# One expert tile is formed in the last batch, and its gate and up products stand between the products of the last routing chain

## The reference

```python
x = norm(x + attention(x, wq, wk, wv, wo, rel_pos))          # 32 heads of 8, a bias by distance
x = norm(x + mamba(ctx_1024, z=x))                           # 16 states, a scan over 256 steps, gated by silu(x)
x = norm(x + ffn(x))

# the third part, for 1024 tokens and 4 experts
probs = softmax(x @ Wr + br); top_w, top_idx = top_k(probs, 1)
h = silu(x @ Wg[e]) * (x @ Wu[e])      # 256 -> 1024, for the token's own expert e
out = (h @ Wd[e]) * top_w              # 1024 -> 256
```

## Time and profile before

| | |
|---|---|
| median of 3 runs | 472.5 us (472.37 to 473.3) |
| the profiled execution, its own time | 473.93 us |
| its span | 472.2 us |
| PE busy | 420.8 us (89%) |
| DVE busy | 312.3 us (66%) |
| POOL busy | 221.1 us (47%) |
| ACT busy | 211.2 us (45%) |
| chain that ended last: PE, DVE, POOL, issue | 66%, 17%, 6%, 5% of the span |

### The profile page before, as it was taken

The page is one execution under the profiler, slowest core; times in us unless marked ns, Lnnn a source line. Parts: engine busy times, 40 slices in busy tenths (PEclk is TensorE's granted clock), DMA queues, the critical chain, the costliest instruction groups (busy, mean ns, idle before and its releaser), DMA issues.

```text
span 472.2 us, 7846 instructions
## 1 busy us (share of the span) xinstructions
PE 420.8 (89%) x2560; PEld 212.2 (45%) x2561; DVE 312.3 (66%) x626; ACT 211.2 (45%) x412; POOL 221.1 (47%) x246
## 2 busy tenths in 40 slices
PE   4989588878998998989989899986999999999993
PEld 3444222333443443444434444354556666666652
DVE  3497778999987878878888786588214333334344
ACT  2456717564664557745577457612121111112220
POOL 2000615877986679967799578600551111111001
PEclk9998765798999999999999999999999999999997
DMA  9689940937365182756324430079120000000000
GB/s 237 91 279 108 301 144 12 146 119 115 89 138 110 68 134 70 134 180 199 137 78 169 159 112 0 1 287 361 55 55 11 12 4 9 11 11 11 11 1 9
DMA packets 39366, 49.36 MB, mean 105 GB/s; under 512 B 4664, under 2 KB 32673, under 8 KB 39334
## 3 DMA queue, kind: packets, MB, share of 16 engines
q1 hardware_dynamic: 36322, 46.65, 39.0%
q0 software_dynamic: 1056, 2.10, 1.5%
q10 hardware_dynamic: 1956, 0.21, 0.4%
HBM read 40.72 MB, written 8.91 MB: 105 GB/s over the span
## 4 chain that ended last, share of the span: by engine, by line
PE 66%; DVE 17%; POOL 6%; issue 5%; DMA 3%; ACT 2%; POOLq 0%; SPq 0%; DVEq 0%; ACTq 0%
PE ps L1181 16%; PE ps L1197 8%; PE ps L883 8%; PE ps L910 6%; PE ps L914 5%; PE ps L956 4%; PE ps L783 4%; DVE arena L1572 3%; DVE arena L1523 3%; DVE arena L1505 3%; PE ps L943 3%; PE ps L1189 2%; DMA arena<-arena 2%; POOL arena L655 2%; POOL arena L661 2%
## 5 line engine op out<-in xcount | busy, mean ns | idle before, releaser
L1372 ACT ACTIVATE arena<-ps 128x512 f32<-128x512 f32 x128 | 76.1, 595 | 84.9 <-PE ps L943 84.7
L1523 DVE TENSOR_REDUCE arena<-ps 128x2 f32<-128x512 f32 x128 | 86.6, 681 | 26.8 <-PE ps L914 22.7
L661 POOL TENSOR_TENSOR arena<-arena 128x512 f32<-128x512 f32 x60 | 76.8, 1279 | 36.2 <-DVE arena L1572 36.2
L655 POOL TENSOR_TENSOR arena<-arena 128x512 f32<-128x512 f32 x64 | 84.4, 1321 | 9.0 <-issue 8.8
L1181 PE MATMUL ps<-arena 128*128 x176 | 77.5, 593 | 0.7 <-ACT arena L1413 0.7
L1572 DVE TENSOR_TENSOR_SCAN arena<-ps,arena 128x512 f32<-128x512 f32 x60 | 72.8, 1214 | 0.5 <-DVE mv L1617 0.2
L883 PE MATMUL ps<-arena,identf 128*128 128x512 f32 x128 | 68.9, 625 | 0.0
L910 PE MATMUL ps<-arena 48*128 48x256 bf16 x256 | 52.7, 288 | 13.4 <-DVE arena L1523 10.0
L1331 ACT ACTIVATE ps<-arena 128x255 f32<-128x255 f32 x128 | 60.4, 473 | 1.9 <-DVEq L1726 1.9
L1839 DVE TENSOR_TENSOR arena<-arena,ps 128x1024 f32<-128x1024 f32 x11 | 13.4, 1222 | 59.9 <-ACT arena L1417 59.9
L731 POOL DMA_INDIRECT out<-rows_s,arena x11 | 10.8, 984 | 88.7 <-DVE rows_s L1868 80.5
(11 more groups left out here) (231 smaller groups left out, 524.7 us busy)
## 6 DMA issues: line engine op xcount, KB each, us to landing
arena<-bc_d SPq DMA_DIRECT2D x32, 512.0 KB, 4.4
arena<-in_L_ffn_Wg SPq DMA_DIRECT2D x8, 512.0 KB, 6.1
arena<-in_L_ffn_Wu SPq DMA_DIRECT2D x8, 512.0 KB, 5.9
arena<-in_L_ffn_Wd SPq DMA_DIRECT2D x4, 1024.0 KB, 11.7
arena<-kp_d SPq DMA_DIRECT2D x8, 384.0 KB, 7.9
arena<-qp_d SPq DMA_DIRECT2D x8, 384.0 KB, 10.8
qp_d<-arena SPq DMA_DIRECT2D x4, 384.0 KB, 8.5
kp_d<-arena SPq DMA_DIRECT2D x4, 384.0 KB, 8.4
```

The lines of the kernel that those rows point to most:

```text
L655: g.tensor_tensor(dBu[m % 3], dtu[:, :, b * SEQ:(b + 1) * SEQ], over_k(bcr[c % BC_RING][:, m % 2, 0, :]), ALU.mult).then_inc(dbu_ready, 1)
L661: g.tensor_tensor(h, h, over_k(bcr[m // 2 % BC_RING][:, m % 2, 1, :]), ALU.mult).then_inc(hc_ready, 1)
L1372: A(prob[2 * (slot % 2) + kt][:, pr * HALF:(pr + 1) * HALF], ps[:, 2 + n % 2, :], ACT.Exp).then_inc(p_ready, 1)
L1523: v.tensor_reduce(negm[b % 2][:, qt, 2 * pair:2 * pair + 2], ps[:, bank, :].rearrange("p (h k) -> p h k", h=2), axis=AX.X, op=ALU.max).the ...
```

## The change

The first two batches hold 4 token tiles, 512 tokens. With 4 experts at least one has 128 or more of them. The change picks the first such expert (`estar`) in the last batch, gives its first 128 tokens slot 0, and routes all other tokens to the slots from 1 on. Slot 0's rows are picked before the end of the routing, and its gate and up are cut into four halves of 4 records each, which stand between the products of the last chain. The number of slots stays 11.

```diff
@@ POOL: the constants stand 7 scans earlier, with 4 memsets more
-                if m == 3 * STATES + 8:
+                if m == 3 * STATES + 1:
                     routing_constants()
-            for s in (1, 0, 2):
+            for s in (2, 0, 1):
                 gather(s)
-            hand_row(1)
+            hand_row(2)
@@ PE
+                        if b == BATCH - 1 and (qd, i) == (3, 0):
+                            count_early()
...
+            pe.wait_ge(y_out, BATCH)
+            pick_rows(EARLY, early_rows, early_ready)
             pe.wait_ge(x2_ready, 2 * (BATCH - 1))
             turn_late(BATCH - 2)
...
-            keep_warm(2, 5)
+            pe.wait_ge(wgu_in, 16 * 16)
+            pe.wait_ge(xcur_ready, 2)
+            first_expert = pe.value_load(estar_int[0:1, 0:1], min_val=0, max_val=EXPERTS - 1)
+            gate_up_half(0, first_expert)
             route_late(BATCH - 1)
-            keep_warm(10, 7)
+            for half in (1, 2):
+                gate_up_half(half, first_expert)
...
             mm(ps[:, 6, 0:EXPERTS * TT], ones_b, oh_cols, start=True, stop=True).then_inc(count_pe, 1)
-            keep_warm(14, 4)
+            gate_up_half(3, first_expert).then_inc(gu_done, 1)
+            keep_warm(4, 4)
...
-            pe.wait_ge(wgu_in, 16 * 16)
-            gate_up(0, first_expert)
-            turn_x(1)
-            keep_warm(8, 6)
             turn_h(0)
@@ ACT
+            take_x(0)
             put_late(0)
@@ DVE, in the last batch
+                        if b == BATCH - 1 and (qd, i) == (2, 1):
+                            dve.wait_ge(taken, turns.count)
+                            early_experts()
+                        if b == BATCH - 1 and (qd, i) == (3, 0):
+                            early_counts()
+                        if b == BATCH - 1 and (qd, i) == (4, 0):
+                            early_choice()
+                        if b == BATCH - 1 and (qd, i) == (5, 0):
+                            early_ranks()
+                        if b == BATCH - 1 and (qd, i) == (6, 0):
+                            early_marks()
@@ DVE, after the loop
+            link(v.tensor_tensor(e_of[:, 0:1], e_of[:, 0:1], estar, ALU.add))
```

More of the change, by code:

```diff
@@ L50 @@
 SLOTS = TT + EXPERTS - 1
+EARLY = TT // 2
 EPS = 1e-5
@@ L1027, in route, with count_early @@
                 last.then_inc(turned, 1)
+            def count_early():
+                pe.wait_ge(early_oh, 1)
+                pe.wait_ge(consts, 4)
+                bank = turn()
+                n = EXPERTS * EARLY
+                mm(ps[:, bank, 0:n].rearrange("p (e t) -> p e t", e=EXPERTS), ltri, ohb[:, :, 0:EARLY], start=True, stop=True)
+                mm(ps[:, bank, n:2 * n].rearrange("p (e t) -> p e t", e=EXPERTS), ones_b, ohb[:, :, 0:EARLY], start=True,
+                   stop=True).then_inc(turned, 1)
             pe.wait_ge(consts, 3)
@@ L1096, in expert_of, with gate_up_half, pick_rows @@
                 return pe.value_load(e_int[0:1, bass.ds(s, 1)], min_val=0, max_val=EXPERTS - 1)
+            def gate_up_half(half, e):
+                w, fh = (wg_s, wu_s)[half // 2], half % 2
+                for k in range(KT):
+                    last = mm(ps[:, half, :], xcur[:, k, :], w[:, bass.ds((e * KT + k) * DFF + fh * HALF, HALF)],
+                              start=(k == 0), stop=(k == KT - 1))
+                return last
+            def pick_rows(tiles, marks, ready):
+                for t in range(tiles):
+                    pe.wait_ge(ready, t + 1)
+                    for k in range(KT):
+                        last = mm(ps[:, 7, k * P:(k + 1) * P], xres[:, t, k * P:(k + 1) * P], marks[t],
+                                  start=(t == 0 and k == 0), stop=(t == tiles - 1), skip_group_check=True)
+                last.then_inc(xt_pe, 1)
             def turn_late(b):
@@ L1147, in _ @@
             mm(ps[:, 6, 0:EXPERTS * TT], ones_b, oh_cols, start=True, stop=True).then_inc(count_pe, 1)
-            keep_warm(14, 4)
+            gate_up_half(3, first_expert).then_inc(gu_done, 1)
+            keep_warm(4, 4)
             pe.wait_ge(x2_ready, TT)
[L1151 to L1156, removed]
+            pick_rows(TT, first_rows, first_ready)
             pe.wait_ge(expert_ready, 1)
-            first_expert = expert_of(0)
             for t in range(TT):
@@ L1177, in gate_up @@
                 pe.wait_ge(xcur_ready, s + 2)
[L1178 to L1183, removed]
+                for half in range(4):
+                    last = gate_up_half(half, e)
                 last.then_inc(gu_done, 1)
@@ L1711, in _ @@
+            def early_marks():
+                for t in range(EARLY):
+                    v.tensor_scalar(early_rows[t], lanes, float(P + 1), lane1[:, t:t + 1], ALU.add,
+                                    ALU.is_equal).then_inc(early_ready, 1)
             dve.wait_ge(ld_route, 32)
```

95 lines of the change are left out of this document (74 added, 21 removed).

## The result

The changed kernel takes 481.27 us (median of 4 runs, 479.62 to 483.43) against 472.75 us (4 runs of the kernel before beside it): a ratio of 1.0182, with an interval of 1.0139 to 1.0226. The forecast was 474.7 us, with a range up to 477.5. The direction was right, the size was not: 8.5 us in place of 2.2.

A forecast was written before the change was run, and what follows sets the result against it. The prediction took the chain to run through PE, and through small DVE operations before 334 us. Batch cost 9.25 less end gain 7.0 made it 2.25 us longer: span 476.2, median 474.7 us, range 467.8 to 477.5.

The forecast's parts named there:

- The gain of the end, 7.0 us: From the routing chain to slot 1: gate and up start at about 338.0, not 345.07; gain between 6.6 and 8.0.
- The conflict: Last batch: small DVE operations wait for POOL's 1.27 us products, so the batch takes 9.25 us, not 3.4; chance 0.45.
- My rule, two inputs in SBUF: Last batch: an inserted DVE operation with both inputs in SBUF lasts until the running POOL product of 1.27 us ends.
- The stalls: Last batch, PE late at inserted DVE work: 2.75 us in quad 2, 1.4 in quad 3, 3.1 in quad 4.
- quads 5 and 6: Last batch: seven operations and four marks take 4.7 us against 2.70 idle on DVE, so 2.0 us late.
- PE is 2.75 us late: Quad 2 of the last batch: the copy ends at 271.2, making PE 2.75 us late in place of 1.0.
- 3.1 us late: Quad 4 of the last batch: the copy ends at 284.6, making PE 3.1 us late in place of 1.0.
- The load of the expert's number takes the place of two fillers and I give it nothing: Routing chain on PE, before the first half's products: the load was priced at zero.
- The signs: Expected in the profile: index to slot 1 2.8 us, counts scan 1.2 us later, PE standing 1.1 us in quad 3.
- 1.2 us of cover: Ahead of the router's products: last Wu lands by 319.1, at most 7.9 us after issue, 1.2 us before PE comes.
- rivals: Small operations free, 468.9, chance 0.27; each mark waits, 476.4, 0.13; all hidden, 465.5, 0.08; others, including late weights, 0.07.
- Each mark waits: Quad 6 of the last batch: each mark waits for its own POOL product, 3.7 us late, 476.4 us; chance 0.13.

The follow-up runs named there:

- 5: Kernel of 2 with a separate semaphore for Wg's loads, so the first half of gate and up waits for Wg alone: 473.10 us, ratio 1.0003.
- 8: Kernel of 7 plus the separate semaphore for Wg's loads and 8 PE fillers ahead of the turn of slot 0: 467.62 us, ratio 0.9889.
- 9: Kernel of 8 with PE's load of the expert's number moved ahead of the 12 fillers: 467.14 us, ratio 0.9864.
- Experiment 3: Changed kernel without four of POOL's products beside the inserted operations of quads 2 and 4: 474.01 us, ratio 1.0039.
- experiment 1: Changed kernel with unused PE filler products ahead of two last-batch waits, 11 in quad 2, 16 in quad 4: 475.46 us, ratio 1.0066.
- 2: Kernel of experiment 1 with 8 more PE fillers ahead of the turn of slot 0: 475.00 us, ratio 1.0046.
- 7: Changed kernel with three groups of its DVE operations moved to places where DVE was idle, constants at m = 52: 470.89 us, ratio 0.9961.
- 6: Changed kernel without its part in the last batch, constants back at m = 56, expert 0 and zero rows for slot 0: 470.76 us, ratio 0.9948.
- experiment 4: Kernel before with only the early routing in the last batch, results unused, old end kept: 485.49 us, ratio 1.0293.

## Why the prediction was wrong

- **The gain of the end, 7.0 us: right as a path, paid late.** With its waits away it is 6.9 (5, 8). In the changed kernel it was 5.9 to the start of slot 1 and 3.9 with the slower products of slot 1. With the load out of the way as well it is 7.9 (9), near the upper bound of 8.0.
- **The conflict: right.** The second inserted operation of quad 2 was to last about 1 us and took 0.74, the third, a copy, 1.19. In quad 4 I named the second and fourth; it was the second and the third, a scalar operation. Experiment 3 shows POOL's products as the cause. My rule, two inputs in SBUF, was too narrow, since the copy and the scalar operation have one. The Trainium skill ("SBUF — State Buffer", section "Who interferes with whom") lists copies and `tensor_scalar` as operations that can enter a two-port mode and contend then; the trace agrees, with 1.19 against 0.17 us.
- **The stalls: right.** Quad 2: the scores start 3.94 us behind the turned maxima in place of 1.30, 2.6 late (forecast 2.75). Quad 3: 0.94 (1.4). Quad 4: 3.54 in place of 0.61, 2.9 late (3.1). That makes 6.5; by experiment 1 it is 7.0 up to the turned maxima of quad 4, where I had 7.25, and 0.3 for all that is behind them, where I had 2.0 for quads 5 and 6. The ranks met no product at all, and DVE's slack hid the marks even at 3.73 us. (In quad 2 the prediction says that six operations remain behind the two that wait; there are seven, and its 270.8 counts seven.)
- **The step that failed: in the terms "PE is 2.75 us late" and "3.1 us late" a stall was priced at its own length.** In the kernel before no stall from the turned maxima of quad 2 to the end of the loop is longer than 0.92 us and its clock is 1.00 there, so I took the products behind a stall at their old duration, and had no rival in which they are slower. Behind 2.58, 3.54 and 1.93 us they ran at the lower clock, and in the batch that was 6.6 us, about as much as the stalls themselves (1). Behind the turn it was 0.9 for the turn and 2.0 for slot 1. The whole difference, for the span: the forecast's chain grew by 2.25 us, the measured one by 9.5. Of these 7.3 us (7.25 before rounding), 6.6 are the clock in the batch, 2.0 the slower slot 1 and 1.1 the end (0.9 of it the slower turn); against them stand 0.2 from the stalls, 1.7 from quads 5 and 6, and the 0.4 us of lead. The Trainium skill ("TensorE: Matmul & The Clock Gate", section "HAM oscillation — how this bites in real kernels") tells of products that start at half the clock behind each wait for a DMA. The trace agrees for the 3.54 us, here a wait for DVE, with 0.59 and 0.55 behind it; behind the 2.41 us of the kernel before nothing of the kind is seen.
- **"The load of the expert's number takes the place of two fillers and I give it nothing": wrong.** It is 0.65 to 0.82 us of PE doing nothing (5, 8), ahead of the products that DVE waits for (9). The fillers that it replaced had been filling idle time; the load stands in the way.
- **The signs.** From the index to gate and up of slot 1 it was to be 2.8 us and is 3.66 (349.00 to 352.66); the turn at the lower clock is the 0.9. The scan of the counts was to be 1.2 us later against the end of the loop: it stands 16.43 us behind the last tail products before and 17.91 after (340.78), 1.5 later. PE was to stand 1.1 us ahead of the tail in quad 3 and stood 0.94.
- **"1.2 us of cover" for Wu: wrong in size.** The wait ahead of the first half was 1.16 us in the changed kernel and 1.99 and 1.86 in 2 and 1; some 0.8 of each is the load. The rest, 0.3 to 1.2, is Wu, and in 5 it goes with the separate semaphore. The longest time from issue to landing on this line was 8.7 us in the changed kernel and 9.6 in 1 and 2, in place of the 7.9 that the cover was reckoned with.
- Of the rivals none had the clock. "Each mark waits" was the nearest in time, and in experiment 1 the four marks did last 3.73 us, three products long. But PE paid little for them, 0.3 us with all else behind quad 4: had the time come out at that rival's 476.4, it would have been luck.

## What to carry to other kernels

Give a new stall of PE two prices: its length, and, as a rival with a chance of its own, the products behind it at the lower of the two clock levels, unless something fills it. Here it came behind 3.54 us and not behind 2.41 us at another place. Read PE's busy share beside PEclk. Before inserting small operations on DVE, look for places where DVE is idle, where POOL has no product running, and where nothing that PE waits for stands behind them: the same 31 operations cost 13.9 us at one set of places and about 1.75 at another. A wait on one semaphore for two groups of loads, and a register load ahead of the products on the critical path, are cheap to take apart, though the gain of each by itself was not clear of the scatter here.

## What the runs showed of the hardware

- A copy and a scalar operation of four numbers a row, with one input in SBUF, wait for the end of a running 128x512 product on POOL: 1.19 us, and 0.17 with POOL's product taken away (3). Beside POOL's memsets the ten operations of quad 2 took 0.16 to 0.20 us (7). Two of the counting operations of quad 3, with one input in PSUM, stood beside a product of POOL in the changed kernel (from 278.84 us) and took 0.17 us each.
- The clock behind a given idle time is not the same in each execution. Behind 0.82 us four records took 1.98 us and behind 0.81 us in another execution of the same kernel 3.40 (9); behind 1.86 us 1.98 and behind 1.26 us 3.56 (1, 3). Behind 1.93 us ahead of the turn it fell each time (the changed kernel, 1, 3, 6, 7). Behind the 2.41 us in the routing chain of the kernel before it did not fall. In experiment 4 the chain is the same and has no stall over 1.43 us, and yet the granted clock was 0.75 in 327 to 335 us. What the chip goes by is not settled here; what PE had done ahead of the idle time differs between these places.
- How long the lower clock lasts differs as well: about 4 us behind the 2.58 us, until 302 us (12 us) behind the 3.54 us, and in experiment 4 less behind about the same stall (0.59 in 287 to 295 us, 1.00 from 295 on).
